# Transfers of 125-row tiles in two pieces, an earlier bias load, and other places for the gate weights in a graph network on one Trainium2 core

## What is computed

```python
xn = layernorm(x)
# layer 0: relational graph convolution, a gate, linear attention
u = xn @ root + bias
for r in range(8):                              # one adjacency matrix for each kind
    u = u + (segment_sum(xn[src] * (kind == r), dst) / max(count_r, 1)) @ weight[r]
z = concat([u, xn]) @ w_gate + b_gate           # w_gate is 2048 x 1024
x = x + tanh(u) * z + xn * (1 - z) + linear_attention(xn, Wq, bq, Wk, bk, Wv, bv, Wo, bo)
# layer 0, second half: four trees of 8 levels route each row to one of 256 leaves
t = normalise(layernorm(x))
q, k, v = tree_q(t), tree_k(t), tree_v(t)       # leaf: relu(t @ w1 + b1) @ w2 + b2
y = t + softmax(q @ k.T / 32) @ v
x = x + y + tree_f(y)
# layer 1
xn = layernorm(x)
x = x + gcn(xn, W, b) + linear_attention(xn, ...)
out = x + ffn(layernorm(x))                     # shared part and 8 experts for 128 chosen rows
```

## Time and profile before

| | |
|---|---|
| median of 3 runs | 2718.56 us (2709.5 to 2718.69) |
| the profiled execution, its own time | 2707.94 us |
| its span in the profile | 2705.8 us |
| PE, busy matmuls | 2399.5 us, 89% |
| DVE, ACT, POOL busy | 51%, 31%, 10% |
| mean granted clock of TensorE | 0.943 |
| moved by DMA | 406.69 MB, mean 150 GB/s |

### The profile page before, as it was taken

How to read it: one execution, slowest core, us unless ns; L and a number is a source line. 1 busy time by engine, 2 the same in 40 slices (tenths; PEclk the granted TensorE clock), 3 DMA queues, 4 the chain that set the end, 5 groups by cost and what they waited for, 6 DMA issues and landing times.

```text
span 2705.8 us, 30851 instructions
## 1 busy us (share of the span) xinstructions
PE 2399.5 (89%) x11841; PEld 1932.6 (71%) x11841; DVE 1392.9 (51%) x2399; ACT 847.9 (31%) x1052; POOL 266.1 (10%) x225
## 2 busy tenths in 40 slices
PE   5899869999999999879889898986869899998996
PEld 4788667777777777657767676865747679876764
DVE  4776234233333333324678776635764233458784
ACT  2232131111111121111167665522644122233441
POOL 3000211000000000010111101001211110202000
PEclk9899989999999999989989998987989999998998
DMA  4145512522221221223598988746854321244882
GB/s 120 58 115 142 145 49 91 159 71 68 74 86 61 81 86 40 86 84 107 217 299 312 313 281 266 269 145 201 296 210 151 122 81 63 91 154 168 278 296 75
DMA packets 170494, 406.69 MB, mean 150 GB/s; under 512 B 71451, under 2 KB 71740, under 8 KB 170320
## 3 DMA queue, kind: packets, MB, share of 16 engines
q1 hardware_dynamic: 143878, 346.61, 38.5%
q0 software_dynamic: 21456, 44.93, 5.5%
q10 hardware_dynamic: 4986, 12.78, 1.6%
HBM read 360.49 MB, written 56.76 MB: 154 GB/s over the span
## 4 chain that ended last, share of the span: by engine, by line
PE 69%; DMA 13%; DVE 9%; issue 4%; ACT 2%; POOL 1%; SPq 1%; DVEq 0%; POOLq 0%; ACTq 0%
PE PS L303 14%; PE PS L304 14%; PE PS L305 14%; PE PS L1141 7%; PE PS L916 4%; DVE low L295 2%; PE PS L1440 2%; DMA q_rows<-leaf_rows_k 2%; PE PS L558 2%; PE PS L1811 2%; PE PS L3040 1%; PE PS L1818 1%; PE PS L1820 1%; PE PS L1819 1%; PE PS L2256 1%
## 5 line engine op out<-in xcount | busy, mean ns | idle before, releaser
L295 DVE TENSOR_TENSOR low<-raw,high 128x1024 fp32r<-128x1024 f32 x467 | 559.9, 1238 | 183.5 <-ACT high L283 180.5
L283 ACT ACTIVATE high<-raw 128x1024 fp32r<-128x1024 f32 x476 | 484.5, 1056 | 403.0 <-PE PS L305 257.4
L303 PE MATMUL PS<-high,xt_high 128*125 128x512 f32 x1280 | 522.6, 408 | 57.5 <-DVE low L295 21.8
L304 PE MATMUL PS<-low,xt_high 128*125 128x512 f32 x1280 | 515.0, 402 | 0.0
L305 PE MATMUL PS<-high,xt_low 128*125 128x512 f32 x1280 | 512.5, 400 | 0.0
L303 PEld LDWEIGHTS PS<-high,xt_high 128*125 128x125 f32 x1280 | 243.5, 190 | 122.6 <-issue 18.2
L305 PEld LDWEIGHTS PS<-high,xt_low 128*125 128x125 f32 x1280 | 243.2, 190 | 63.5
L304 PEld LDWEIGHTS PS<-low,xt_high 128*125 128x125 f32 x1280 | 243.8, 190 | 58.2
L1165 ACT ACTIVATE y_high<-PS 125x512 fp32r<-125x512 f32 x80 | 47.8, 598 | 502.3 <-PE PS L305 502.3
L1176 DVE TENSOR_TENSOR y_low<-PS,y_high 125x512 fp32r<-125x512 f32 x80 | 55.3, 692 | 284.6 <-ACT y_high L1165 284.6
L1141 PE MATMUL PS<-y_high,a_kind 125*125 125x512 f32 x400 | 158.5, 396 | 2.2 <-DVE u_rows L1183 2.2
(11 more groups left out here) (514 smaller groups left out, 3879.9 us busy)
## 6 DMA issues: line engine op xcount, KB each, us to landing
raw<-in_L_ffn_ew SPq DMA_DIRECT2D x96, 512.0 KB, 5.7
raw<-in_L_gnn_weight SPq DMA_DIRECT2D x64, 512.0 KB, 5.7
raw<-in_L_ffn_k_w SPq DMA_DIRECT2D x64, 512.0 KB, 6.7
raw<-in_L_ffn_q_w SPq DMA_DIRECT2D x64, 512.0 KB, 11.4
...
```

Of the source, the lines that this page charges most:

```text
L283: a.e.activation(high_of(i)[:, 0:w], RAW[PLACE_OF[i]][:, 0:w], ACT.Copy).then_inc(*a.step(part_high, 1, [("high", i)]))
L295: v.e.tensor_tensor(LOW[p][:, 0:w], RAW[p][:, 0:w], high_of(i)[:, 0:w], ALU.subtract).then_inc(*v.step(signal, 1, [("low", i)]))
L303: p.e.matmul(dst, xh[:, kt, xs], wh[:, c], start=first and j == 0, stop=False)
L304: p.e.matmul(dst, xh[:, kt, xs], wl[:, c], start=False, stop=False)
```

## The change

1. A helper `move_rows` issues a 125-row transfer as two DMAs, rows 0 to 111 and rows 112 to 124, which signal one semaphore. It takes the place of the one DMA in the transfers of tiles: 116 more DMAs on SP's queue (the ten a_tile loads leave it, so it has 106 more in all), 20 more on ACT's (q_rows and gnn_row), 8 more on POOL's (a_kind). Bias rows that are spread to all partitions, a_tile and the stores of POOL (x_root, x_mixed) stay whole.
2. bias_q is loaded near the start of POOL's queue, and the five loads of the counts no longer wait for each other.
3. The gate's first parts go to the ring of the relations (ring 57 now reaches to part 115), and four of its loads (parts 110 to 113) stand before x_tile with no wait for the adjacency store; the rest of the rings is renumbered. The x_tile tiles and bias_g lie in a_sum's memory, and x_tile is loaded when the adjacency stores and the degree sums are done, not among the gate's parts.
4. The degrees are made after the last at_stage, not before the first.
5. POOL, not SP, loads a_tile (x + attention) in the gate stage.

```diff
-    AFTER_K, ROUTED, BASE = [23, 24], [25, 26, 27, 28], [3, 4, 5, 6, 7, 8, 9, 10]
-    LEAVES, BESIDE = [9, 10, 0, 1, 2, 3, 4, 5, 6, 7, 8], [29, 30]
+    AFTER_K, ROUTED, BASE = [23, 24], [25, 26, 27, 28], [6, 9, 0, 1, 2, 10, 7, 8]
+    LEAVES, BESIDE = [7, 8, 3, 4, 5, 6, 9, 0, 1, 2, 10], [29, 30]
     RINGS = [(0, EARLY + [12, 13]),
              (11, BESIDE + [2, 3, 4, 5, 6, 12, 13, 0, 1]),
              (24, [2, 3, 4, 5, 6, 12, 13, 0, 1]),
              (57, [11, 13, 0, 1, 2, 3, 4, 5, 6, 12]),
-             (107, [7, 8, 9, 10, 0, 1, 2, 3, 4, 5, 6]),
+             (116, [9, 0, 1, 2, 7, 8, 3, 4, 5, 6, 9, 0, 1, 2, 10]),
              (131, LEAF_K + LEAF_Q + LAST + LEAVES),
              (200, LEAF_Q + LAST + LEAVES),
              (250, LEAVES),
-             (329, AFTER_K + LAST + [0, 1] + ROUTED + [2] + BASE),
-             (369, LAST + [0, 1, 2] + BASE)]
+             (329, AFTER_K + LAST + [3, 4] + ROUTED + [5] + BASE),
+             (369, LAST + [3, 4, 5] + BASE)]
...
+    def move_rows(x, out, in_, sem, *key):
+
+        x.e.dma_start(out[0:112], in_[0:112]).then_inc(*x.step(sem, 16, []))
+        x.e.dma_start(out[112:PT], in_[112:PT]).then_inc(*x.lands(sem, *key))
...
         e.iota(bsti[:, :], [[128, NB]], base=0, channel_multiplier=0).then_inc(*g.mark())
+        mixer_gpsimd(g, M0)
...
-            g.wait_ge(g.before(cnt_sem))
             e.dma_start(rc[:, j, :], cntd[:, j * PT:(j + 1) * PT].rearrange("r p -> p r"), allow_slow_non_contiguous=True).then_inc(*g.lands(cnt_sem, "counts in", j))
...
-            s.e.dma_start(XN[:, t, :], A["x"][t * PT:(t + 1) * PT, :]).then_inc(*s.lands(xsem[t], "x in", t))
+            move_rows(s, XN[:, t, :], A["x"][t * PT:(t + 1) * PT, :], xsem[t], "x in", t)
...
     def degrees_vector(v):
-        v.wait_ge(at("target iota"))
-        v.e.tensor_copy(tgt[:, :], tgti[:, :]).then_inc(*v.mark())
-        v.wait_ge(at("kinds", 7, 4))
-        v.e.tensor_reduce(deg[:, :], ASUM[:, :, :], axis=AX.X, op=ALU.add).then_inc(*v.mark())
+        v.e.tensor_reduce(deg[:, :], ASUM[:, :, :], axis=AX.X, op=ALU.add).then_inc(*v.mark("degree sums"))
...
-        v.wait_ge(*[at("counts in", j) for j in range(TT)])
+        v.wait_ge(at("counts in", TT - 1))
...
                 if n == 75:
+                    v.wait_ge(at("target iota"))
+                    v.e.tensor_copy(tgt[:, :], tgti[:, :]).then_inc(*v.mark())
+                turn_sum_vector(v, n - 75)
+                if n == 79:
                     degrees_vector(v)
-                turn_sum_vector(v, n - 75)
             elif n > 9:
...
             s.wait_ge(s.before(xsem[t]))
-            s.e.dma_start(U[:, t, :], rootd[t * PT:(t + 1) * PT, :]).then_inc(*s.lands(xsem[t], "root in", t))
-        load_parts(s, 107, *[at("acc stored", n) for n in (7, 8, 9)])
+            move_rows(s, U[:, t, :], rootd[t * PT:(t + 1) * PT, :], xsem[t], "root in", t)
+        load_parts(s, 110, *[at("acc stored", n) for n in (7, 8, 9)])
         for j in range(TT):
             turn_sum_sync(s, j)
-        load_parts(s, 115, at("adjt stored", 4))
...
-    XG = [place(f"x_tile{i}", [PT, D], F32, LENT + 4096 * i) for i in range(2)]
-    BG = place("bias_g", [PT, D], F32, LENT + 8192)
+    XG = [place(f"x_tile{i}", [PT, D], F32, SPARE + 4096 * i) for i in range(2)]
+    BG = place("bias_g", [PT, D], F32, SPARE + 12288)
...
+    def load_acc(g, n):
+        h, t = divmod(n, TT)
+        g.wait_ge(at("x1", n - 4) if n > 3 else at("u", 79), g.before(aps[n % 4]))
+        g.e.dma_start(AP_[n % 4][:, :], acc[t * PT:(t + 1) * PT, 512 * h:512 * h + 512]).then_inc(*g.lands(aps[n % 4], "acc in", n))
+
     def gates_gpsimd(g):
+        for n in range(4):
+            load_acc(g, n)
         for t in range(TT):
             g.wait_ge(g.last, at("tanh", t), at("xg", t))
             g.e.tensor_tensor(U[:, t, :], U[:, t, :], XG[t % 2][:, :], ALU.subtract).then_inc(*g.mark("delta", t))
-
-    def load_acc(s, n):
-        h, t = divmod(n, TT)
-        if n > 3:
-            s.wait_ge(at("x1", n - 4))
-        else:
-            s.wait_ge(at("agg", 79), at("u", 79))
-        s.wait_ge(s.before(aps[n % 4]))
-        s.e.dma_start(AP_[n % 4][:, :], acc[t * PT:(t + 1) * PT, 512 * h:512 * h + 512]).then_inc(*s.lands(aps[n % 4], "acc in", n))
+        for n in range(4, 10):
+            load_acc(g, n)
 
     def gates_sync(s):
-        s.wait_ge(*[at("used", i) for i in lent(LAST, 107)])
-        s.e.dma_start(BG[:, :], A["L0_gnn_b_gate"].partition_broadcast(PT)).then_inc(*s.lands(bg_sem, "bias g"))
-
         def load_x(t):
             if t > 1:
                 s.wait_ge(at("delta", t - 2))
             s.wait_ge(s.before(xgs[t % 2]))
-            s.e.dma_start(XG[t % 2][:, :], A["x"][t * PT:(t + 1) * PT, :]).then_inc(*s.lands(xgs[t % 2], "x tile", t))
-
-        load_x(0)
-        load_x(1)
-        load_parts(s, 119)
-        load_x(2)
-        for n in range(4):
-            load_acc(s, n)
-        load_x(3)
-        load_acc(s, 4)
-        load_x(4)
-        for n in range(5, 8):
-            load_acc(s, n)
-        load_parts(s, 123)
-        load_acc(s, 8)
-        load_parts(s, 127)
...
+            move_rows(s, XG[t % 2][:, :], A["x"][t * PT:(t + 1) * PT, :], xgs[t % 2], "x tile", t)
+
+        load_parts(s, 114)
+        s.wait_ge(at("adjt stored", 4), at("degree sums"))
+        for t in range(2):
+            load_x(t)
+        s.e.dma_start(BG[:, :], A["L0_gnn_b_gate"].partition_broadcast(PT)).then_inc(*s.lands(bg_sem, "bias g"))
+        for t in range(2, TT):
+            load_x(t)
+        load_parts(s, 120)
+        load_parts(s, 130, at("delta", 4))
...
-        load_acc(s, 9)
...
-        load_parts(s, 131)
+        load_parts(s, 131, at("z out", 1, 4))
...
-        a.e.dma_start(QA[n % 2][:, :], yb[f][t * PT:(t + 1) * PT, :]).then_inc(*a.lands(collect_sem[n % 2], "collected", f, t))
+        move_rows(a, QA[n % 2][:, :], yb[f][t * PT:(t + 1) * PT, :], collect_sem[n % 2], "collected", f, t)
...
-            s.e.dma_start(out[t * PT:(t + 1) * PT, :], SO[:, t, :]).then_inc(*s.lands(x3s[t], "out", t))
+            move_rows(s, out[t * PT:(t + 1) * PT, :], SO[:, t, :], x3s[t], "out", t)
```

More of the change, by code:

```diff
@@ L1075, in mix0_sync @@
         for t in range(TT):
-            s.e.dma_start(XB[:, t, :], A["x"][t * PT:(t + 1) * PT, :]).then_inc(*s.lands(xbs[t], "x again", t))
+            move_rows(s, XB[:, t, :], A["x"][t * PT:(t + 1) * PT, :], xbs[t], "x again", t)
         for h in range(2):
@@ L2707, in back @@
                 a.wait_ge(a.before(sgs[j % 4]))
-                e.dma_start(w[:, :], x2d[j * PT:(j + 1) * PT, 512 * h:512 * h + 512]).then_inc(*a.lands(sgs[j % 4], "x2 back", h, j))
+                move_rows(a, w[:, :], x2d[j * PT:(j + 1) * PT, 512 * h:512 * h + 512], sgs[j % 4], "x2 back", h, j)
         a.wait_ge(at("shift", 0))
```

39 lines of the change are left out of this document (19 added, 20 removed).

## The result

The changed kernel takes 2554.36 us (median; 2553.05 to 2556.23), the kernel before 2715.06 us in the runs beside it: ratio 0.941, 95% interval 0.9389 to 0.9432. The forecast was 2553.

A forecast was written before the change was run, and what follows sets the result against it. PE's idle time, mostly waits for DMA, with 125-row tiles on about 5 of 16 engines, was taken as the bound. Twelve terms sum to 163 us, giving 2545 or 2556 by starting point, put at 2553; range 2508 to 2612.

The forecast's parts named there:

- The split tile: 125-row transfers: 112 rows spread over 16 engines, 1.35 us a tile for 3.88; bounds nothing or 2.5 us saved.
- over 300 GB/s: Sign in the profile after: windows with only 125-row tiles moving show this rate and a share near 1.00.
- q_rows: Leaf stage, ACT's tile loads: the whole 22.9 us of four waits and a little clock, 24 us (12 to 28).
- bias_q: Attention's q bias, loaded behind five count loads: issued early, it ends the wait for q_tmp, 31 us (28 to 32).
- Gate: Gate stage: shorter waits for low halves and ut_low, plus fuller clock, 34 us in sum (24 to 40).
- the third case of the rivals: Two pieces move no faster than one; bias_q, gate order and some clock leave 53 us, 2666; chance 0.05.
- I leave 4 of the 7.6: Gate's first part: its low half stands behind the degrees on DVE, so 4 us of that wait stay.
- Issues at nothing: SP's queue: 116 extra issues, some 40 us, priced at nothing, with up to 6 us where SP is late.
- f back: x_tile wait when f returns: first tile 2.5 us earlier, later ones at POOL's pace, 8 us (5 to 12).
- A landing of its own for the second piece: The 13-row piece lands 3.9 us later for 31 tiles: 68 us slower, 2787; chance 0.02.
- Late weights in the leaf stages: Weights late in turn take the gain of q_rows and the first gather: 2581; chance 0.20.
- A stall of the new rings: A weight part waits for a ring place still used, a loss of any size; chance 0.01.

The follow-up runs named there:

- e3_cut64: The changed kernel with each tile cut at row 64, into 64 and 61 rows: 3450.76 us, ratio 1.2713.
- e8_cut100: The changed kernel with each tile cut at row 100, into 100 and 25 rows: 2588.65 us, ratio 0.954.
- e4_bias_only: The kernel before with only the load of bias_q moved to the start of POOL's queue: 2681.03 us, ratio 0.9877.
- e2_whole: The changed kernel with its helper issuing the 125 rows as one DMA again, all else kept: 2663.8 us, ratio 0.9813.
- e1_split_only: The kernel before with only the transfers written as two pieces by move_rows: 2590.55 us, ratio 0.9542.
- e5_x1_first: The changed kernel with SP loading leaf weights 126 to 129 behind the first x1 and xn1 stores, not ahead of them: 2539.58 us, ratio 0.9354.
- e6_pool_holds: The changed kernel with POOL's four adds x + f held until DVE has made the shift of tile 0: 2553.77 us, ratio 0.941.
- e9_q_rows_only: The kernel before with only the ten q_rows loads of ACT's queue in two pieces: 2686.29 us, ratio 0.9907.

## Why the prediction was right, and where not

**What bounds it.** Held. PE's waits for DMA, directly or through DVE and ACT, were what the change could win, and the clock went along: 124 us of gaps and 30 of busy time.

**The split tile.** The direction held (e3_cut64, e8_cut100), the price did not: "1.35 us in place of 3.88" is 1.98 (512,000 B at 259 GB/s), and the sign "over 300 GB/s" did not come. The saving lies between the two bounds, 1.9 us, and I took the upper one, 2.5. That the sum came out all the same no run explains, and it is in part luck: the pace of a tile still counts, since from 2.7 us a tile (e8_cut100) to 2.0 the span fell by 31.7, so terms such as q_rows (27.3 where its wait and clock were put at 24) were priced too low for a tile at 1.35.

**bias_q**: 31 forecast, 32.7 measured, 32.6 by the shift of e4_bias_only. Nothing behind it was late in its place.

**Gate**: 34 forecast, 33.5 measured, of which e2_whole gives 33.4 by the order alone. The terms that I put down to faster tiles were its work too: the third case of the rivals had "about 20" for the order without them. Its total of 53 met e2_whole all the same (2666 forecast, 2663.8 measured), since the 20.5 lost at x1, which it did not have, stand against that. The step "I leave 4 of the 7.6" for the degrees: 3.5 was left. The clock gave 4.3 of the 7 taken, by the busy time of the same 194 matmuls (48.1 to 43.8 us).

**Issues at nothing.** "116 of them are some 40 us of a queue that mostly waits for places of the ring, so I price them at nothing" held for the issues, as far as e1_split_only shows (its shift falls at no end of a stage of the table), but the step left out what the moved weight loads do in that queue. I had followed the gate's parts to x_tile and POOL's queue behind a_tile, not the x1 stores behind parts 126 to 129. The forecast had no term there; it was -15.5, and e5_x1_first, which moves the stores ahead, gives all of it back.

**f back**: 8 forecast, 4.5 measured. The step that failed is "DVE is busy 12.09 of the 19 us, so its chain stays". The chain went from 7.0 to 11.7 us, because the tiles came faster and POOL's adds stood beside it. Taking that away (e6_pool_holds) moved the wait to the next tiles and won nothing in the whole, so the 3.5 us that are missing are not shown to come from the chain alone.

**The others.** Start, adjacency, v, x again, x2 back, x_back and out came within 4 us each. The rest of attention (2.8) had no term, and the gather gave 3.2 in place of 7. The sum of 163 met 154.6 of span: the misses at x1, f back and the gather, 23 us together, were partly made up by q_rows, x again, x_back, out, the bias and the attention stage, each 1.6 to 3.4 us above its term. That 2553 met 2554.36 to 1.4 us is luck: the sum was 8 us too high, and the two starting points for it, 2707.94 and 2718.56, lie 10.6 apart.

**The rivals.** Two pieces at one piece's speed: out, shares of 1.0, so the sentence of the Trainium skill that the prediction quotes, "Don't bother", does not hold for 112 and 13 of 125 rows. A landing of its own for the second piece: out, since tiles in a stream are 2.0 us apart and not later than before. Late weights in the leaf stages: out (e9_q_rows_only). "A stall of the new rings" had 0.01 as a loss of the whole; a stall of that kind did come, of 15 us.
